# The D skip of a state-space layer by transposes of x·D from ScalarE, and the state's product moved next to the tile's own product

## The reference, cut to what matters

```python
xn = layernorm(x)
# state-space branch (per tile of tokens; 4 heads of 64 channels)
z, x, Bg, Cg, dd_dt, dd_A, trap, angles = split(xn @ W_in)
theta = cumsum(angles * dt)                      # angles of the rotation
K = rope(rmsnorm(Bg) * w + B_bias, theta); Q = rope(rmsnorm(Cg) * w + C_bias, theta)
y  = (scores(Q, K) * decay) @ x                  # inside the tile
y += (Q * exp(ell)) @ H                          # with the state H before it
y  = y + D * x                                   # the skip, one D per head
out1 = (y * silu(z)) @ W_out
# expert branch: for each token its two experts
h = silu(xn @ W1[e]) * (xn @ W3[e]); out2 += w * layernorm(h @ W2[e])
out = input + out1 + out2
```

## Time and profile before

| | us |
|---|---|
| median of 3 runs | 292.38 (290.68 to 293.24) |
| the profiled execution | 291.83 |
| its span in the trace | 289.8 |

### The profile page before, as it was taken

The page is one execution under the profiler, slowest core; times in us unless marked ns, Lnnn a source line. Parts: engine busy times, 40 slices in busy tenths (PEclk is TensorE's granted clock), DMA queues, the critical chain, the costliest instruction groups (busy, mean ns, idle before and its releaser), DMA issues.

```text
span 289.8 us, 7396 instructions
## 1 busy us (share of the span) xinstructions
PE 257.9 (89%) x2187; PEld 224.2 (77%) x2190; DVE 228.8 (79%) x623; ACT 134.2 (46%) x428; POOL 214.8 (74%) x292
## 2 busy tenths in 40 slices
PE   2999958789999999999999999999999999999700
PEld 0758835688898899889978988997899889988600
DVE  4688997577868968897978898888969896976536
ACT  2765987424445344635254434355253635343023
POOL 8668997828888888897888798878888784765400
PEclk9999999779999999999999999999999999999975
DMA  5631905975779877977878788788787978860095
GB/s 154 205 102 34 340 2 160 312 226 155 233 218 268 269 229 216 281 232 230 275 234 237 243 242 251 238 246 252 215 269 238 267 242 251 247 201 31 18 273 162
DMA packets 68855, 61.55 MB, mean 212 GB/s; under 512 B 6608, under 2 KB 52304, under 8 KB 68816
## 3 DMA queue, kind: packets, MB, share of 16 engines
q1 hardware_dynamic: 66256, 55.83, 64.3%
q0 software_dynamic: 2560, 5.25, 6.3%
HBM read 56.27 MB, written 4.78 MB: 211 GB/s over the span
## 4 chain that ended last, share of the span: by engine, by line
PE 73%; DVE 9%; POOL 5%; ACT 4%; issue 3%; DMA 3%; SPq 1%; POOLq 0%; ACTq 0%; DVEq 0%
PE bank L859 20%; PE bank L900 10%; PE bank L854 5%; PE bank L803 5%; PE bank L795 4%; PE bank L818 3%; PE bank L896 3%; PE bank L783 3%; PE bank L769 3%; PE bank L787 2%; PE bank L812 2%; PE bank L774 2%; PE bank L836 2%; DMA decay<-res_dram 2%; POOL blk L576 2%
## 5 line engine op out<-in xcount | busy, mean ns | idle before, releaser
L859 PE MATMUL bank<-blkT,w_up 128*128 128x128 f32 x512 | 66.1, 284 | 2.1 <-DVE xrow L1366 2.1
L859 PEld LDWEIGHTS bank<-blkT,w_up 128*128 128x128 f32 x512 | 62.0, 196 | 5.2 <-issue 2.6
L624 POOL DMA_INDIRECT res_dram<-xrow,sidx x40 | 40.9, 1022 | 15.2 <-DVE xrow L1394 10.9
L576 POOL DMA_INDIRECT blk<-xn_dram,gidx x40 | 45.6, 1139 | 8.7 <-issue 7.6
L1063 ACT ACTIVATE xrow<-bank 128x512 f32<-128x512 f32 x40 | 24.7, 618 | 32.6 <-PE bank L859 29.6
L900 PE MATMUL bank<-w,xrow 128*128 128x128 f32 x256 | 35.5, 283 | 0.3 <-DVE xrow L1381 0.3
L900 PEld LDWEIGHTS bank<-w,xrow 128*128 128x128 f32 x256 | 32.0, 196 | 1.6 <-issue 1.6
L1298 DVE SCALAR_TENSOR_TENSOR kq<-sd,rms,bias_kq 128x512 f32<-128x512 f32 x32 | 23.3, 766 | 11.5 <-POOL rms L591 11.0
L1366 DVE TENSOR_TENSOR xrow<-xrow,bank 128x512 f32<-128x512 f32 x40 | 27.1, 678 | 6.6 <-PE bank L859 6.5
L617 POOL TENSOR_TENSOR rstd<-mv,mhalf 128x1 f32<-128x1 f32 x40 | 26.8, 670 | 3.8 <-DVE mv L1378 3.4
L1057 ACT ACTIVATE blkT<-bank 128x128 f32<-128x128 f32 x40 | 11.7, 293 | 31.0 <-PE bank L845 31.0
(11 more groups left out here) (242 smaller groups left out, 611.8 us busy)
## 6 DMA issues: line engine op xcount, KB each, us to landing
w_up<-in_L_ffn_W_dram SPq DMA_DIRECT2D x96, 256.0 KB
w<-in_L_ffn_W_dram SPq DMA_DIRECT2D x48, 256.0 KB, 3.8
e_row<-e_dram SPq DMA_DIRECT2D x16, 256.0 KB, 4.5
decay<-l_dram SPq DMA_DIRECT2D x4, 512.0 KB, 5.3
gam<-in_L_ffn_gamma_dram SPq DMA_DIRECT2D x32, 64.0 KB
shift_y<-in_L_ffn_beta_dram SPq DMA_DIRECT2D x32, 64.0 KB
acc<-in_L_attn_u_dram SPq DMA_DIRECT2D x4, 256.0 KB, 4.0
xn_dram<-xrow SPq DMA_DIRECT2D x4, 256.0 KB, 5.6
```

Source lines behind the costliest of these rows:

```text
L576: g.indirect_dma_start(out=blk[:, b % SLOTS, :], out_offset=None, in_=xn_dram, in_offset=bass.IndirectOffsetOnAxis(ap=gidx[:, entry(b):ent ...
L624: g.indirect_dma_start(out=res_dram, in_=res[:, b % HALF, :], in_offset=None, out_offset=bass.IndirectOffsetOnAxis(ap=sidx[:, entry(b):ent ...
L859: last = m(bank[out][:, c * P:(c + 1) * P], w_up[:, u % SETS, n, c * P:(c + 1) * P], blkT[:, b % 2, :], start=True, stop=True)
```

## The change

- The skip no longer comes from `w_skip`. ScalarE makes `x_d`, x times D, by four scaled copies from PSUM in `gates` (two buffers in turn), and `inter` transposes it into bank 3, one instruction for each of the two halves. GpSimd's product for `w_skip` goes. `project_x` waits for these copies as well, because they read its bank.
- `inter` stands behind `rise(b1)` and `turn_h`, directly ahead of `intra`.
- The absolute value of the angles moves from VectorE (`token`) to ScalarE (`sines`, an `Abs` ahead of the two `Sin`).
- VectorE's `fade` moves from ahead of `rotate` to behind it.

```diff
-            pool.wait_ge(rest_in, 16 * RESTS)
-            g.tensor_tensor(w_skip[:, :].rearrange("p (h d) -> p h d", d=HD),
-                            w_in[:, DI:2 * DI].rearrange("p (h d) -> p h d", d=HD), bc(dskip[:, :], HD, 1), ALU.mult)\
-                .then_inc(skip_ready, 1)
...
             def project_x(t):
                 again(pe, s["x_ready"], t)
                 again(pe, s["xs_ready"], t)
+                again(pe, s["xd_ready"], t)
...
             def inter(u):
                 again(pe, s["acc_done"], u)
-                pe.wait_ge(skip_ready, 1)
+                pe.wait_ge(s["xd_ready"], u + 1)
                 for c in range(2):
-                    m(bank[3][:, c * P:(c + 1) * P], w_skip[:, c * P:(c + 1) * P], xnT[:, u * P:(u + 1) * P],
-                      start=(c == 0), stop=False)
+                    m(bank[3][:, c * P:(c + 1) * P], x_d[:, u % 2, 2 * c:2 * c + 2, :].rearrange("p h d -> p (h d)"),
+                      ident[:, :], is_transpose=True, start=(c == 0), stop=False)
...
                     turn_block(b0 + 2)
-                if second:
-                    inter(t - 1)
                 if b1 is not None:
                     rise(b1)
                     turn_h(b1 - 1)
                 if second:
+                    inter(t - 1)
                     intra(t - 1)
...
             def sines(t):
-                act.wait_ge(s["ang_ready"], t + 1)
+                act.wait_ge(theta_ready, t // TB + 1)
+                a(ang[:, :], theta[:, t, :], ACT.Abs).then_inc(s["ang_ready"], 1)
                 again(act, s["k_rot"], 2 * t)
                 again(act, s["rot_pool"], 2 * t)
                 a(trig[:, 0, :, :].rearrange("p h n -> p (h n)"), theta[:, t, :], ACT.Sin, scale=TWO_PI)
+                act.wait_ge(s["ang_ready"], t + 1)
...
                 a(tile, tile, ACT.Silu).then_inc(s["gate_ready"], 1)
-                act.wait_ge(s["x_psum"], t + 1)
+                again(act, s["inter_psum"], t - 1)
+                for h in range(NH):
+                    last = a(x_d[:, t % 2, h, :], bank[0][:, h * HD:(h + 1) * HD], ACT.Copy, scale=dskip[:, h:h + 1])
+                last.then_inc(s["xd_ready"], 1)
...
-            def token(t):
-
-                again(dve, s["trig_ready"], t)
-                th = theta[:, t, :]
-                stt(ang[:, :], th, -1.0, th, ALU.mult, ALU.max).then_inc(s["ang_ready"], 1)
...
                     rot_cosine(t)
-                if second and first:
-                    fade(t - 1)
                 if first:
                     rotate(t)
                 if second and first:
+                    fade(t - 1)
                     carry(t - 1)
```

More of the change, by code:

```diff
@@ L137, in build @@
         qs = sb("qs", [P, NH * P])
-        w_skip = sb("w_skip", [P, DI])
+        x_d = sb("x_d", [P, 2, NH, HD])
         state = sb("state", [P, NH, HD])
@@ L277, in build @@
             "z_psum", "z_ready", "turns_cut", "lg_read", "tot_psum"))
-        g_ready, lng_ready, wstate_ready, lnw_ready, rows_cut, arm_psum, skip_ready, decay_ready, own_ready, decay_done = (
-            sem(n) for n in ("g_ready", "lng_ready", "wstate_ready", "lnw_ready", "rows_cut", "arm_psum", "skip_ready", "decay_ready", "own_ready",
+        g_ready, lng_ready, wstate_ready, lnw_ready, rows_cut, arm_psum, decay_ready, own_ready, decay_done = (
+            sem(n) for n in ("g_ready", "lng_ready", "wstate_ready", "lnw_ready", "rows_cut", "arm_psum", "decay_ready", "own_ready",
                              "decay_done"))
         names = ("x_psum bc_psum sq_done ms_ready rms_ready k0_ready q0_ready ang_ready"
-                 " trig_ready rot_dve rot_pool k_rot kT_psum qT_psum kT_ready qT_ready"
+                 " trig_ready xd_ready rot_dve rot_pool k_rot kT_psum qT_psum kT_ready qT_ready"
                  " score_psum sd_ready x_ready xs_ready gate_ready qs_ready inter_psum intra_psum state_psum bcw_ready"
@@ L1284, in _ @@
             diagonal(0)
-            token(0)
             def mean_square(t):
@@ L1401, in iteration @@
                     dve.wait_ge(rest_in, 16 * RESTS)
-                if first and t > 0:
-                    token(t)
                 if b0 is not None:
```

## The result

The changed kernel takes 288.98 us (median of nine runs, 287.36 to 289.75) against 292.38 for the kernel before (nine runs, 290.32 to 293.24): a ratio of 0.9882, with a 95% interval of 0.9849 to 0.9915. It is 1.2% faster; the forecast was 287.3, 1.7% less, with a range of 284.2 to 290.5. The profiled execution took 287.36 with a span of 285.6, so the span is 4.2 us shorter than before, where 5.1 were forecast. Of the nine executions three, the profiled one among them, have spans of 285.6 to 286.2 us at a mean granted clock of 0.963 to 0.968, and six have 286.9 to 288.0 at 0.955 to 0.958.

The account below looks back on a forecast made before the run. TensorE's row bounds the loop, even passes also VectorE's chain to the gate; 8 x 0.78 less 7 x 0.16 makes 5.1 us off 291.83, 286.7, plus 0.55 for the median: 287.3, range 284.2 to 290.5.

Parts of the forecast that it names:

- TensorE's row: TensorE's sequence of instructions per pass was to get shorter by 0.51 us in even passes and 0.78 in odd ones.
- 0.09 + 32 x 0.0625 = 2.09: Odd pass on TensorE: time in us for 32 narrow instructions in one run without a seam, entry cost included.
- TensorE goes first, and 0.78 is kept: Odd pass, transposes of Q: TensorE arrives at 8.97 after project_bc, the gate allows 8.84, so 0.78 us is saved.
- Even passes are bound twice: Even passes are bound by TensorE's row and by the chain from project_bc through norm and rotation to the gate.
- Everything behind it on VectorE is queued: Copies delay the first block's Silu, VectorE's product starts 0.16 us late, and the gate TensorE waits for is equally late.
- Rival B: The product's delay is swallowed or more by less overlap with `own_sq`: gain 6.2 to 9.8, 286.2 to 282.6 us; chance 0.19.
- Both ahead of it, so for Q nothing changes: 0: VectorE's `fade` behind `rotate`: the gate still has both operations ahead of it, so the effect counts 0.
- `token`, `Abs`: 0: Taking `token` off VectorE and putting `Abs` on ScalarE ahead of `squares` shortens nothing in the chain: 0.
- A: ScalarE's copies cost more than four in a row did; at 0.326 us each, 1.7 us slower, 294.1; chance 0.07.
- C: GpSimd takes over as bound in odd passes, each saving only 0.4: gain 2 us, 290.3; chance 0.13.
- D: The clock falls in passes with the new wait; one stretch in each of three passes takes the gain away, 292.4; chance 0.04.
- E: Transposes of `x_d` into an accumulating bank cost as much as the products; gain 3.3 us, 289.1; chance 0.07.

Follow-up runs that it names:

- e7_skip_only: Kernel before with only the skip changed (four ScalarE copies, two transposes instead of products): 289.28 us, ratio 0.9891.
- e6_order_only: Kernel before with only TensorE's order changed, `inter` moved behind the second up-projection, skip still by products: 287.15 us against 292.02, ratio 0.9848.
- e2_late_copies: Changed kernel with ScalarE's `x_d` and `x_w` copies moved behind the first block's Silu: 287.59 us, ratio 0.9893 against the kernel before.
- e9_copies_only: Kernel before with the four ScalarE copies added, their result used by nothing, `project_x` waiting for them: 292.48 us, ratio 1.0002.
- e1_fade_back: Changed kernel with `fade` put back ahead of `rotate` on VectorE: 285.35 us against 290.31 for the kernel before, ratio 0.9805.
- e8_abs_only: Kernel before with only the absolute value of the angles moved from VectorE to ScalarE: 291.47 us, ratio 1.0001.
- e4_gate_first: Changed kernel with `fade` ahead of `rotate` and the gate ahead of `carry`: 283.25 us, ratio 0.9727 against the kernel before.
- e13_changed_own_later: Changed kernel with only GpSimd's `own_sq` moved behind the gather for the second block: 288.1 us, run once, no ratio.
- e10_own_later: Changed kernel with `fade` ahead of `rotate` and `own_sq` behind the second block's gather: 292.49 us against 290.79 for the kernel before, ratio 1.0039.

## Why the prediction was right, and where its reasons were not

- **TensorE's row: right.** Skip 0.23 (15.42 to 15.19 in `e7_skip_only`), the up-projection 1.79, the even row 11.01 for 11.05. Mis-sized was one term, "0.09 + 32 x 0.0625 = 2.09": it measured 1.90. In even passes the up-projection takes 2.01, not 1.79, while the copies delay the Silu ahead of it. The bare odd row is 14.43, not 14.64.
- **"TensorE goes first, and 0.78 is kept" (odd pass): right in size by luck, wrong in reason.** The row was 0.99 shorter, TensorE did not go first, and the gate took 0.21 back.
- **Even passes are bound twice: right.** `e6_order_only` shortens their row and they stay at about 11.56.
- **"Everything behind it on VectorE is queued", 0.16 late at the gate: the step that failed.** The product was 0.23 late, and the rotation's products beside `own_sq` gave it all back (`e2_late_copies`, `e9_copies_only`). Rival B described this; it was given 0.19 as a whole and would have left the even pass at 11.56 or less.
- **"Both ahead of it, so for Q nothing changes: 0" (`fade`): the other step that failed.** The count of instructions is unchanged, but their neighbours are not, and it costs 0.31 and 0.13 (`e1_fade_back`). The two errors cancel in part in the even pass: +0.16 was forecast, +0.29 came, 7 x 0.13 = 0.9 us, the whole gap between 5.1 and 4.2.
- **`token`, `Abs`: 0, right** (`e8_abs_only`).
- **Rivals A, C, D, E: none came.** A: four copies took 0.78. C: in the waits after, TensorE waits for GpSimd only once, ahead of the loop. E: the transposes of `x_d` cost 0.22. D: the loop's windows have a granted clock of 1.00, with more transposes in them and a wait in each even pass. The Trainium skill ("TensorE: Matmul & The Clock Gate", part 4) says that a transpose does not count as TensorE being busy in the same way; with the transposes added here the trace shows no fall of the clock.

By medians the gain was 3.4 us, by spans 4.2. The forecast put the median 0.55 above the profiled execution, as before; with the change it lies 1.6 above. So of the 1.7 between 287.3 and 288.98 only a part belongs to the mechanism. In which stage the slower executions lose time is not shown; no trace shows them.

Open: why a VectorE operation that needs the one ahead loses 0.11 in one place and 0.19 in the other, and whether it is the data or the wait for the other's semaphore, which the kernel has in both places; why the even passes of `e6_order_only` and `e7_skip_only` vary between 11.5 and 11.8, and what the single long passes are (12.46 in `e9_copies_only`, 14.88 in `e4_gate_first`). A place for `own_sq` at which VectorE reads no two operands from SBUF was not tried, nor `e4_gate_first` without the skip's copies.

## What to carry to other kernels

Where a pass is bound twice, a shorter row of the bounding engine gives nothing until the other chain is cut as well: one moved call (`e6_order_only`) brought about what the whole change did, all of it in the odd passes, and reordering VectorE's chain on top of the change (`e4_gate_first`) brought 2.7% against 1.2%. Don't price a reordering by counting instructions ahead of a wait; look at which now depends on its direct neighbour, and put an independent one between the two. A delay that enters a stretch where an operation is longer than its bare length may end there, so price it by the end of that stretch, and test a "free" edit by undoing it alone.

## What the runs showed of the hardware that was not expected

- Two VectorE operations of 128x256 follow each other at 0.33 to 0.34 us, each 0.42 long, when the second does not need the first. When it does and waits for its semaphore, the step was 0.45 (rotation's product, 165.78, to `rotate`, 166.23, in `e13_changed_own_later`) and 0.52 (`fade` to `carry`): 0.11 to 0.19 more. In pass t=15 of the changed kernel, which has no `own_sq`, the steps are 0.45 and 0.52 as well; in that of the kernel before they are 0.34 and 0.33.
- GpSimd's `own_sq` (128x512, 0.70 us) took between 0.44 and 0.92 us from VectorE operations of 0.42 that read two operands from SBUF, whichever they were: 0.71 and 0.85 together before, 0.43 and 0.85 after, 1.34 in `e10_own_later`, 0.89 in `e13_changed_own_later`. In the last, a bare `fade` would have ended 0.2 before the record of `own_sq` begins. So the start shown for `own_sq` seems to be later than its effect, or the end of the DMA issue ahead of it takes part; this is not shown. Operations with one operand in PSUM kept their length beside GpSimd's two sine parts (0.68 for `mask` at 3.98 to 4.66 after `project_bc`, before; a sine part runs from 4.02 to 4.75).
- Narrow instructions of 64 columns come at 0.055 us each once in a run (L824 and L893: 24 in 1.31), and the first 8 take 0.59, so entering the group costs 0.15. By that a run of 16 would take 1.03; the piece of 16 at 1.09, from which the forecast took its 0.09 and 0.0625, was 0.06 longer, for a reason that is not shown. Leaving costs 0.15 even in front of a single transpose (0.26 for L842, where L842 takes 0.11 behind full-width products).
